# Attention in a four-layer kernel: q and k turned once and gathered by DMA, outputs moved by DMA in turned form

## The chip, the cores and the metric

One core of a Trainium2 chip runs the whole program. The metric is the device time of one execution in microseconds (us); the number for a kernel is the median of its runs.

## The reference, cut to what matters

The program chains a mixture-of-experts layer, an attention layer, a second mixture-of-experts layer, a sparse feed-forward layer, a state-space layer ("ssm" in the names) and a second sparse feed-forward layer on 1024 tokens of width 256. The change touches the attention and the preparation of the state-space layer.

```python
# attention on normalized x: 32 query heads, 8 key/value heads, head width 8
q = x @ Wq.T ; k = x @ Wk.T ; v = x @ Wv.T
q, k = rope(q, k)
scores = einsum('bkgqd,bkld->bkgql', q, k) * 8 ** -0.5
attn = softmax(scores, axis=-1)
out = einsum('bkgql,bkld->bkgqd', attn, v)
x = x + out.reshape(b, s, 256) @ Wo.T
```

## The kernel before

`attention_layer` (L597) works on 8 tiles of 128 tokens. Every product of q and k is made in split precision: a value is a high part (rounded for TensorE) and a low part, and both stand as rows of one operand, so that a contraction over 32 rows (`STACK`) gives hi·hi + lo·hi + hi·lo and, for the second pass, minus the row maximum (its two parts meet rows of −1 in k). Two heads lie in 64 rows; in `kz` ("k_picks") the rows of the head that is not wanted are zero.

Preparation: TensorE projects a tile, VectorE applies the rotation (L846 to L850), ScalarE copies the rounded parts into `q_stack` and `k_stack` (`stack_high`, L948), GpSimd subtracts the low parts (L781, L783). k is turned for all heads at once (L1037) and copied to `kT` (L960).

The main part goes over 8 groups (one key/value head and its 4 query heads each), written out for groups 0 and 7 and as a loop for 1 to 6. A group has 16 slots. In a slot TensorE issues, in this order: two transposed score matmuls (`scoresT`, L1103) into one pair of banks, two score chunks (L1087), two `scoresT` into the other pair, one chunk, the four value matmuls of the slot before (`values`, L1115), one chunk. ScalarE takes the exponential of each pair (L981, two of 128x1024 per slot). VectorE takes the row maximum of each chunk (`reduce`, L863), 4 a slot; these belong to rows that are needed later, since the second pass needs the maximum of the first. The chunks run ahead: `LEAD` = 40 chunks of group 0 are made before slot 0, and each group makes the rest of its own and the first 40 of the next. Chunks and turned things share a ring of three PSUM banks, given out by the table `bank_of`; TensorE waits until the holder of a bank is read.

In each group six jobs of four 128x128 transposes stand in that order too (`slot_jobs`, inserted as fourth job, behind the value matmuls): "q1" at slots 3 and 4 (L1063: the next group's q for the score chunks, copied by ScalarE, L965), "q2" at slots 6 and 14 (L1063: q with its maxima, copied by L969), and "o" at slots 1 and 9 (L1123: the output of half a group back to token order; VectorE then takes reciprocals of the sums, L871, and multiplies, L876). GpSimd splits the maxima into two parts (L804, L806) and copies each group's q (L787). SyncE gathers a group's k with 4 DMAs (L755). After group 7 the outputs are turned once more, split, projected with `w_o` and added (`turn_final`, `project_final`, L1135 to L890).

In `prepare` of the state-space layer each of 8 groups has two convolutions; ScalarE does the first tap (L1509), VectorE three more (L1514), TensorE the projections of the next group (L62 to L64), for which ScalarE rounds the weights (`high`, L1712) and GpSimd subtracts (`low`, L1641).

## Time and profile before

| what | value |
|---|---|
| median of 3 runs | 1743.71 us (1729.76 to 1744.64) |
| the profiled execution's own time | 1740.03 us |
| its span in the trace | 1738.2 us |
| mean granted TensorE clock | 0.932 of full speed |
| TensorE / VectorE / ScalarE / GpSimd busy | 86 / 62 / 50 / 28 % of the span |

All times in the trace count from the span's start. The attention runs from 193 to 674 us, the preparation of the state-space layer from 961 to 1066 us. A row of the timeline joins neighbouring instructions of one group (its count stands behind x); in square brackets stands how long the engine was idle before it and what ended that.

### The profile page before, as it was taken

The page shows a single profiled execution, that of the slowest core. Times are in us where ns is not written, and L with a number is a line of the kernel's source. Part 1 is how long each engine was busy: PE and PEld are TensorE (multiplying, and loading weights), DVE is VectorE, ACT ScalarE, POOL GpSimd, SP SyncE. Part 2 cuts the span into 40 slices and gives each one's busy share as a digit, 9 for nine tenths or more (in the row PEclk, how much of TensorE's full clock was granted, in tenths as well). Part 3 has the DMA queues.
Part 4 walks back from the last instruction along what each step waited for, and adds up shares of the span by engine and source line. Part 5 has one row for each costly group of instructions (what it writes and reads, how often), then busy time and mean ns, then how long its engine had stood idle before and what let it go on. Part 6 is the DMA issues. An engine that isn't in the chain of part 4 may idle for free. (4 is left out here: it accounts for less than half of the span.)

```text
span 1738.2 us, 24514 instructions
## 1 busy us (share of the span) xinstructions
PE 1488.4 (86%) x7880; PEld 1033.9 (59%) x7880; DVE 1080.0 (62%) x1948; ACT 877.6 (50%) x1268; POOL 493.8 (28%) x422
## 2 busy tenths in 40 slices
PE   3999479899998996799499787799999999999697
PEld 2566343333333334466277675688888888888586
DVE  4121577787888754212277665778777777878375
ACT  1222226676676673122143566666766666675332
POOL 1344320000000000244210112466565555565200
PEclk7999759999999997799799898999999999999799
DMA  8432210000000004623400111223232222331200
GB/s 299 122 49 40 50 25 1 13 13 12 12 12 0 12 1 153 216 43 49 104 11 1 43 34 49 88 76 100 70 99 92 73 91 73 102 93 46 76 1 25
DMA packets 78526, 107.33 MB, mean 62 GB/s; under 512 B 9600, under 2 KB 57984, under 8 KB 78432
## 3 DMA queue, kind: packets, MB, share of 16 engines
q1 hardware_dynamic: 69056, 91.98, 16.8%
q0 software_dynamic: 9376, 14.16, 4.6%
q8 instruction: 51, 0.84, 0.2%
q14 instruction: 43, 0.35, 0.1%
HBM read 89.99 MB, written 11.93 MB: 59 GB/s over the span
## 5 line engine op out<-in xcount | busy, mean ns | idle before, releaser
L981 ACT ACTIVATE attn_probs<-attn_scoresT 128x1024 f32<-128x1024 f32 x256 | 253.3, 1024 | 101.5 <-PE attn_scoresT L1103 99.0
L863 DVE TENSOR_REDUCE attn_max_chunks<-attn_scores 128x1 f32<-128x512 f32 x349 | 227.7, 685 | 48.7 <-PE attn_scores L1087 48.7
L1514 DVE SCALAR_TENSOR_TENSOR ssm_scan_x<-ssm_scan_proj,ssm_w_conv,ssm_scan_x 128x1023 f32<-128x1023 f32 (+2 forms) x96 | 123.0, 1282 | 80.8 <-ACT ssm_scan_x L1509 75.0
L1087 PE MATMUL attn_scores<-attn_k_picks,attn_qT_pass 64*128 64x512 f32 x349 | 149.8, 473 | 25.8 <-DVE attn_max_chunks L863 17.0
L1103 PE MATMUL attn_scoresT<-attn_qT_pass,attn_k_picks 64*128 64x512 f32 x512 | 163.9, 438 | 0.7 <-ACT attn_probs L981 0.7
L401 DVE TENSOR_TENSOR moe_h<-moe_silu,moe_up 128x512 f32<-128x512 f32 x46 | 31.6, 688 | 189.4 <-PE moe_up L516 189.4
L1115 PE MATMUL attn_o<-attn_probs,attn_v_group 128*32 128x512 f32 x1024 | 139.0, 615 | 0.9 <-ACT attn_probs L981 0.8
L1087 PEld LDWEIGHTS attn_scores<-attn_k_picks,attn_qT_pass 64*128 64x128 f32 x349 | 63.0, 192 | 122.6 <-DVE attn_max_chunks L863 98.2
L448 ACT ACTIVATE moe_silu<-moe_gate 128x512 f32<-128x512 f32 x46 | 27.5, 598 | 200.4 <-PE moe_gate L516 200.4
L62 PE MATMUL ssm_scan_proj<-ssm_xnT_hi,ssm_w_in_hi 128*128 128x512 f32 x256 | 108.7, 425 | 23.0 <-DVE ssm_scan_x L1514 21.0
L286 POOL DMA_INDIRECT moe_sums<-moe_y,moe_token x46 | 72.8, 1583 | 165.6 <-DVE moe_y L410 159.4
L2351 PE MATMUL ssm_scan_out<-ssm_scan_w_out,ssm_scan_v 128*128 128x256 f32 x480 | 113.5, 391 | 4.6 <-POOL ssm_scan_w_out L2056 4.4
L863 DVE TENSOR_REDUCE attn_max_chunks<-attn_turn 128x1 f32<-128x512 f32 x139 | 94.5, 680 | 28.0 <-PE attn_turn L1087 28.0
L64 PE MATMUL ssm_scan_proj<-ssm_xnT_hi,ssm_w_in_lo 128*128 128x512 f32 x256 | 102.6, 401 | 0.0
L2351 PEld LDWEIGHTS ssm_scan_out<-ssm_scan_w_out,ssm_scan_v 128*128 128x128 f32 x480 | 92.3, 197 | 17.2 <-POOL ssm_scan_w_out L2056 4.6
L63 PE MATMUL ssm_scan_proj<-ssm_xnT_lo,ssm_w_in_hi 128*128 128x512 f32 x256 | 102.3, 399 | 0.0
L804 POOL TENSOR_TENSOR attn_q_group<-attn_max,attn_zeros 128x16 fp32r<-128x16 f32 x16 | 3.6, 228 | 336.3 <-DVE attn_max L857 336.3
L2241 ACT ACTIVATE ssm_scan_gate<-ssm_scan_v 128x1024 f32<-128x1024 f32 x24 | 25.4, 1058 | 137.7 <-DVE ssm_scan_v L2134 137.7
L2034 POOL TENSOR_TENSOR ssm_scan_c_exp_cum<-ssm_cT,ssm_scan_exp_cum 128x896 f32<-128x896 f32 x32 | 70.8, 2212 | 80.9 <-PE ssm_scan_y L2325 79.5
L516 PE MATMUL moe_gate<-moe_w_gate_up,moe_xT 128*128 x184 | 90.3, 614 | 1.3 <-ACT moe_xT L442 1.3
L546 PE MATMUL moe_out<-moe_w_down,moe_hT 128*128 x368 | 87.1, 380 | 1.5 <-ACT moe_hT L454 1.5
L2042 POOL TENSOR_TENSOR ssm_scan_x_to_end<-ssm_scan_x_dt,ssm_decay_to_end 128x512 f32<-128x512 f32 x64 | 87.6, 1387 | 1.8 <-DVE ssm_scan_x_dt L2098 1.8
(337 smaller groups left out, 3415.2 us busy)
## 6 DMA issues: line engine op xcount, KB each, us to landing
ssm_cum_all<-ssm_cums SPq DMA_DIRECT2D x32, 512.0 KB, 3.8
ssm_scan_exp_cum<-ssm_cums SPq DMA_DIRECT2D x32, 512.0 KB, 3.7
moe_w_gate_up<-in_moe_w SPq DMA_DIRECT2D x16, 512.0 KB, 10.8
moe_w_up<-in_moe_w SPq DMA_DIRECT2D x16, 512.0 KB, 10.9
moe_w_down<-in_moe_w SPq DMA_DIRECT2D x16, 512.0 KB, 11.1
ssm_w_in<-in_in_w SPq DMA_DIRECT2D x64, 128.0 KB, 2.6
attn_k_picks<-attn_kT SPq DMA_DIRECT2D x32, 128.0 KB, 2.4
ssm_scan_w_out<-in_out_w SPq DMA_DIRECT2D x8, 512.0 KB, 3.9
```

The source lines that it names most:

```text
L62: nc.tensor.matmul(out, lhs_hi, rhs_hi, start=start, stop=False)
L63: nc.tensor.matmul(out, lhs_hi, rhs_lo, start=False, stop=False)
L64: return nc.tensor.matmul(out, lhs_lo, rhs_hi, start=False, stop=stop)
L516: last = nc.tensor.matmul(bank[:].unsqueeze(1), xT[i % 2][:, k, :], w_in[name][:, bass.ds(e * KD + k, 1), :], start=(k == 0), stop=(k == K ...
L863: return nc.vector.tensor_reduce(rmaxc[:, half, place:place + 1], chunk_bank(g, n), AX_X, ALU.max).then_inc(reduced, 1)
L981: nc.scalar.activation(probs[s % 2][:, 2 * pair:2 * pair + 2, :], st_ps[pair][:], ACT.Exp, scale=SCALE).then_inc(exp_done, 1)
L1087: nc.tensor.matmul(chunk_bank(g, n), qm[b][head_rows(j), t * P:(t + 1) * P], kz[b][head_rows(j), j % 2, c * BANK:(c + 1) * BANK], start=Tr ...
L1103: last = nc.tensor.matmul(st_ps[pair][:, i, :], kz[b][head_rows(j), j % 2, kt * P:(kt + 1) * P], qe[b][head_rows(j), half * BANK:(half + 1 ...
L1115: last = nc.tensor.matmul(o_ps[j * STACK:(j + 1) * STACK, :], vg[b][:, kt, :], probs[s % 2][:, i, :], start=(kt == 0), stop=(kt == KT_TILE ...
L1514: return nc.vector.scalar_tensor_tensor(out[:, shift:], ps[:, :S - shift], w(k), out[:, shift:], ALU.mult, ALU.add)
L2042: nc.gpsimd.tensor_tensor(xend[:, cs, :], xdt[:, cs, :], to_end[:, cs, bass.ds(n, 1)] .broadcast_to([P, cs.stop - cs.start, PD]), ALU.mult ...
L2351: last = nc.tensor.matmul(out[:, m, :], v[:, v_row(b * NORM_HEADS + jn), cols], w_out[:, jn, :], start=(jn == 0), stop=(jn == NORM_HEADS - 1))
```

## The change

q and k are turned to `[head rows, tokens]` once, in the preparation, straight from the rotated tiles (`turn_roped`, three transposes a tile), rounded and split there by half of the tokens (`turned_high`, `turned_late` on ScalarE, `turned_parts` on VectorE, one subtraction on GpSimd). SyncE then gathers a group's rows with DMAs: 12 for k, 6 for q, and 2 that clear the rows of the maxima (`load_group`). The two passes use one operand `qs` ("q_group"); the maxima alone are turned in the loop, as one transpose of 128x32 (`turn_max`), copied by VectorE (`copy_max`) and put into `qs` by two DMAs (`load_max`). The outputs stay turned: ScalarE copies them to `oT`, and 8 DMAs of 8 rows each (`send_out`) put values and sums into `o_all` and `o_sums`. The division is done at the end, for 4 blocks of 128x512 (or 96x512): reciprocal and rounding on VectorE, product and low part on GpSimd; the last group still goes by the old way. `LEAD` becomes 44, the order of chunks within a half changes, and the slots of the last projections move from 13 and 14 to 11 and 13. In `prepare` of the state-space layer `high` of the next group stands before the `silu` and the second tap.

```diff
 TURNS = (0, 2, 1, 3)
-FINAL_SLOTS = (11, 12)
 PER_SLOT = CHUNKS // SLOTS
-LEAD = HALF + 2 * PER_SLOT
+LEAD = HALF + 3 * PER_SLOT
 LEAD_SCORES_T = 36
+LEAD_MAX = LEAD_SCORES_T + 2
+OWN_TOP_SLOT = (CHUNKS - LEAD) // PER_SLOT - 1
+NEXT_TOP_SLOT = (CHUNKS + HALF - LEAD) // PER_SLOT - 1
+FINAL_SLOTS = (11, 13)
+LAST_ROWS = 3 * STACK
...
+            c, r = divmod(r, HALF // 2)
+            return TURNS[r % GQ], half * (TT // 2) + r // GQ, c
...
-            if s in Q1_SLOTS:
-                jobs.insert(3, ("q1", 1, Q1_SLOTS.index(s)))
-            if s == KT_TILES - 2:
-                jobs.insert(3, ("q2", 0, 1))
-            if s == SLOTS - 2:
-                jobs.insert(3, ("q2", 1, 0))
-            if s == 1:
-                jobs.insert(3, ("o", -1, 1))
-            if s == KT_TILES + 1:
-                jobs.insert(3, ("o", 0, 0))
+            if s == OWN_TOP_SLOT + 1:
+                jobs.append(("max", 0, 1))
+            if s == NEXT_TOP_SLOT + 1:
+                jobs.append(("max", 1, 0))
             return jobs
...
+            def load_group(g):
+                b = g % 2
                 if g >= 2:
                     sync.wait_ge(scoresT_done, 2 * SLOTS * (g - 1))
+                if g >= 4:
+                    sync.wait_ge(hi_done, 6)
+                    sync.wait_ge(q1_lo, 2)
+                load_k(g, kT_hi, (0, 1), slice(0, S), kz_in[b])
+                load_k(g, kT_lo, (3,), slice(0, S), kz_in[b])
+                load_q(g, qT_hi, (0, 3), slice(0, S), q_in[b])
+                load_q(g, qT_lo, (1,), slice(0, S), q_in[b])
+                if g >= 2:
+                    for w in range(2):
+                        at = w * SPAN + STACK
+                        sync.dma_start(f32(qs[b][at:at + 4, :]), none[:]).then_inc(q_in[b], 16)
+
+            def load_max(g, half):
+                sync.wait_ge(m_copied, 2 * g + half + 1)
+                for w in range(2):
+                    at = w * SPAN + STACK
+                    sync.dma_start(f32(qs[g % 2][at:at + 4, half_cols(half)]),
+                                   f32(topsT[half][w * 16:(w + 1) * 16, :])).then_inc(max_in[half], 16)
+
+            def send_out(g, half):
+                sync.wait_ge(o_copied, 2 * g + half + 1)
                 for j in range(GQ):
-                    src = (g % 4) * STACK
-                    sync.dma_start(f32(kz[g % 2][j * STACK:(j + 1) * STACK, j % 2, :]),
-                                   f32(kT[src:src + STACK, g // 4, :])).then_inc(kz_in[g % 2], 16)
+                    row = g % 4 * STACK + j * HD
+                    for dst, at in ((o_all, j * STACK), (o_sum, j * STACK + HD)):
+                        sync.dma_start(dst[row:row + HD, g // 4, half_cols(half)], oT[half][at:at + HD, :]
+                                       ).then_inc(o_out[half], 16)
+
...
+                load_q(0, qT_lo, (1,), half_cols(half), q_first[half])
+            load_max(0, 0)
+            for g in range(KV):
+                if g < KV - 1:
+                    load_group(g + 1)
+                if g:
+                    send_out(g - 1, 1)
+                load_max(g, 1)
+                if g < KV - 1:
+                    send_out(g, 0)
+                    load_max(g + 1, 0)
...
+                half, k = divmod(u, KD)
+                rows, cols = slice(0, LAST_ROWS if k else P), half_cols(half)
+                pool.wait_ge(rec_done, u + 1)
+                nc.gpsimd.tensor_tensor(o_all[rows, k, cols], o_all[rows, k, cols], o_sum[rows, k, cols], ALU.mult
+                                        ).then_inc(prod_done, 1)
+                pool.wait_ge(prod_hi, u + 1)
+                nc.gpsimd.tensor_tensor(oT_lo[rows, k, cols], o_all[rows, k, cols], f32(oT_hi[rows, k, cols]), ALU.subtract
...
+                dve.wait_ge(m_turned, 2 * g + half + 1)
+                if not (isinstance(g, int) and g == 0):
+                    dve.wait_ge(max_in[half], 32 * g)
+                nc.vector.tensor_copy(topsT[half][:], max_bank(g, half)[0:STACK, 0:P]).then_inc(m_copied, 1)
+
+            def reciprocals(k, half):
+                rows, cols = slice(0, LAST_ROWS if k else P), half_cols(half)
+                dve.wait_ge(o_out[half], 16 * 2 * GQ * (KV - 1))
+                nc.vector.reciprocal(o_sum[rows, k, cols], o_sum[rows, k, cols]).then_inc(rec_done, 1)
...
+                dve.wait_ge(prod_done, KD * half + k + 1)
+                nc.vector.tensor_copy(oT_hi[rows, k, cols], o_all[rows, k, cols]).then_inc(prod_hi, 1)
...
+            def last_slot(s):
+
+                if s == OWN_TOP_SLOT + 2:
+                    reciprocals(0, 0)
+                    reciprocals(1, 0)
+                    high_parts(0, 0)
+                    high_parts(1, 0)
+                if s == KT_TILES + 1:
+                    last_outputs(0)
+                if s == KT_TILES + 2:
+                    last_low(0)
+                    reciprocals(0, 1)
+                    high_parts(0, 1)
+                if s == KT_TILES + 4:
+                    reciprocals(1, 1)
+                    high_parts(1, 1)
...
+            def turned_high(half):
+                rows, cols = slice(0, KV * HD), half_cols(half)
+                act.wait_ge(turned, 3 * half + 1)
+                nc.scalar.copy(kT_hi[:, cols], k_bank[half][rows, :]).then_inc(hi_done, 1)
+                act.wait_ge(turned, 3 * half + 2)
+                nc.scalar.copy(qT_hi[:, 0, cols], q_bank[half]).then_inc(hi_done, 1)
...
+                if not (isinstance(g, int) and g == 0):
+                    act.wait_ge(o_out[half], 16 * 2 * GQ * g)
+                nc.scalar.copy(oT[half][:], o_ps[:]).then_inc(o_copied, 1)
...
+                pe.wait_ge(roped_done, t + 1)
+                parts = ((k_bank[half][0:KV * HD, cols], roped[:, t, HEADS * HD:]), (q_bank[half][:, cols], roped[:, t, 0:P]),
+                         (q1_bank[half][:, cols], roped[:, t, P:2 * P]))
+                for dst, src in parts:
+                    last = nc.tensor.transpose(dst, src, ident)
+                    if t % 4 == 3:
...
+            def turn_max(g, half):
                 pe.wait_ge(top_split, 2 * g + half + 1)
-                turn_q(q2_bank(g, half), b, half, q2_turned)
-
...
+            def group_ready(g, b):
+                pe.wait_ge(kz_in[b], 96 * g if b == 0 else 96 * (g - 1) + 192)
+                pe.wait_ge(q_in[b], 64 * g if b == 0 else 64 * (g - 1) + 96)
...
+                            turn_o(0)
+                        if s == KT_TILES + 2:
+                            turn_final(0)
                         for p in range(2):
                             if s == FINAL_SLOTS[p]:
-                                turn_final(p)
-                            if s == FINAL_SLOTS[p] + 2:
                                 project_final(p)
...
             def body(g, b):
                 first, last = edge(g)
                 tap(g, 0)
+                if not last:
+                    high(g + 1, 1 - b)
                 if not first:
                     silu(g - 1, 1 - b, 1)
                 tap(g, 1)
-                if not last:
```

On TensorE, one slot of group 1 with a turn. Before, slot 3 (L1063 is the "q1" job, `attn_turn` the third bank of the ring):

```order
L1087 MATMUL attn_scores<-attn_k_picks,attn_qT_pass_1 128x512
L1109 REGISTER_ALU
L1115 MATMUL attn_o<-attn_probs,attn_v_group 32x512 x4
L1047 REGISTER_ALU
L1068 REGISTER_ALU
L1063 MATMUL attn_turn<-main_ident,attn_q_group 128x128 x4
L1047 REGISTER_ALU
L1087 MATMUL attn_scores<-attn_k_picks,attn_qT_pass_1 128x512
L1099 ISA
L1103 MATMUL attn_scoresT<-attn_qT_pass_1,attn_k_picks 128x512 x2
```

And in the changed kernel, slot 5, the first of the two slots of a group in which something is turned (`attn_max_parts` are the split maxima):

```order
L1147 MATMUL attn_scores<-attn_k_picks,attn_q_group 128x512
L1169 REGISTER_ALU
L1175 MATMUL attn_o<-attn_probs,attn_v_group 32x512 x4
L1116 REGISTER_ALU
L1147 MATMUL attn_scores<-attn_k_picks,attn_q_group 128x512
L1116 REGISTER_ALU
L1126 REGISTER_ALU
L1127 MATMUL attn_scores<-main_ident,attn_max_parts 32x128
L1159 ISA
L1163 MATMUL attn_scoresT<-attn_q_group,attn_k_picks 128x512 x2
```

Four transposes between the value matmuls and the fourth chunk have become one, behind the fourth chunk; the slots with "q1" and "o" turn nothing now.

On SyncE, what the whole attention issues before:

```order
L743 DMA attn_w_qkv<-in_w_qkv 128x2x384
L744 DMA attn_cos<-in_cos 128x8x4
L745 DMA attn_sin<-in_sin 128x8x4
L746 DMA attn_w_o<-in_w_o 128x2x256
L755 DMA attn_k_picks<-attn_kT 32x1024 x32
```

And in the changed kernel, the start of what it issues for group 1 (the load of group 2, then the outputs of half a group):

```order
L749 DMA attn_k_picks<-attn_kT_hi 8x1024 x8
L749 DMA attn_k_picks<-attn_kT_lo 8x1024 x4
L757 DMA attn_q_group<-attn_qT_hi 16x1024 x4
L757 DMA attn_q_group<-attn_qT_lo 16x1024 x2
L774 DMA attn_q_group<-attn_no_max 4x1024 x2
L788 DMA attn_o_all<-attn_oT 8x512
L788 DMA attn_o_sums<-attn_oT 8x512
```

The last two stand four times; then come the 2 DMAs of the maxima (L780), again 8 of outputs and 2 of maxima: 40 a group where there were 4.

On ScalarE, one group of the state-space preparation (group 2), before:

```order
L1509 ACTIVATE ssm_prep_conv<-ssm_prep_proj,ssm_b_conv,ssm_w_conv 128x1024
L1749 ACTIVATE ssm_prep_cT_first<-ssm_prep_conv 128x128
L1750 ACTIVATE ssm_cT<-ssm_prep_conv 128x896
L1509 ACTIVATE ssm_prep_conv<-ssm_prep_proj,ssm_b_conv,ssm_w_conv 128x1024
L1712 CAST ssm_prep_w_bc_hi<-ssm_prep_w_bc 128x512
```

and in the changed kernel:

```order
L1572 ACTIVATE ssm_prep_conv<-ssm_prep_proj,ssm_b_conv,ssm_w_conv 128x1024
L1775 CAST ssm_prep_w_bc_hi<-ssm_prep_w_bc 128x512
L1812 ACTIVATE ssm_prep_cT_first<-ssm_prep_conv 128x128
L1813 ACTIVATE ssm_cT<-ssm_prep_conv 128x896
L1572 ACTIVATE ssm_prep_conv<-ssm_prep_proj,ssm_b_conv,ssm_w_conv 128x1024
```

The rounding of the next group's weights has moved past the second tap and the two `silu` instructions.

## Rows read from the trace of the kernel before

**Rows 1.** Stretches: length, busy PE, PEld, DVE, ACT, POOL, PEclk, DMA share, GB/s.

```profile
232.00:258.00 26.00, 21.52 (x43) 10.36 (x43) 22.45 (x39) 1.46 (x2) 1.66 (x3) 0.50 0.08 17
310.00:360.00 50.00, 45.12 (x279) 17.68 (x271) 40.36 (x69) 34.58 (x38) 2.36 (x6) 1.00 0.05 11
```

**Rows 2.** Timeline of group 0: value matmuls (L1115) and a "q1" turn.

```profile
270.83 1.06 PE L1115 MATMUL attn_o<-attn_probs,attn_v_group 128*32 128x512 f32 x8
271.83 0.66 PE L1063 MATMUL attn_turn<-main_ident,attn_q_group 128*128 128x128 f32 x4
274.73 1.06 PE L1115 MATMUL attn_o<-attn_probs,attn_v_group 128*32 128x512 f32 x8
...
278.61 1.07 PE L1115 MATMUL attn_o<-attn_probs,attn_v_group 128*32 128x512 f32 x8
281.31 1.07 PE L1115 MATMUL attn_o<-attn_probs,attn_v_group 128*32 128x512 f32 x8
```

**Rows 3.** Timeline: an "o" turn, and the same slot a group later.

```profile
290.23 1.06 PE L1115 MATMUL attn_o<-attn_probs,attn_v_group 128*32 128x512 f32 x8
...
295.01 1.07 PE L1115 MATMUL attn_o<-attn_probs,attn_v_group 128*32 128x512 f32 x8
...
345.88 1.07 PE L1115 MATMUL attn_o<-attn_probs,attn_v_group 128*32 128x512 f32 x8
```

**Rows 4.** Groups by shape: busy us, mean ns of one, idle before.

```profile
L981 ACT ACTIVATE attn_probs<-attn_scoresT 128x1024 f32<-128x1024 f32 x256 | 253.3, 1024 | 101.5 <-PE attn_scoresT L1103 99.0
L863 DVE TENSOR_REDUCE attn_max_chunks<-attn_scores 128x1 f32<-128x512 f32 x349 | 227.7, 685 | 48.7 <-PE attn_scores L1087 48.7
...
L871 DVE RECIPROCAL attn_recip<-attn_scores 128x16 f32<-128x16 f32 x15 | 3.7, 249 | 8.0 <-PE attn_scores L1123 8.0
...
L316 DVE RECIPROCAL moe_rstd<-moe_std 128x4 f32<-128x4 f32 x4 | 0.7, 178 | 2.3 <-ACT moe_std L427 2.3
```

**Rows 5.** Line L755, the gather of k: issue ns min/median/max, and landing.

```profile
L755 SPq DMA_DIRECT2D attn_k_picks<-attn_kT x32: 507/591/1600, 227.8 to 567.0; - x32
...
DMA to landing us min/median/max: 2.3/2.4/3.5
```

**Rows 6.** Timeline of the preparation and the lead of the attention.

```profile
210.05 0.49 DVE L850 TENSOR_TENSOR attn_roped<-attn_qk_cos,attn_qk_sin 128x320 f32<-128x320 f32 x1
...
211.35 0.73 POOL L783 TENSOR_TENSOR attn_q_stack<-attn_roped,attn_q_stack 128x256 f32<-128x256 f32 x1
211.44 0.99 DVE L850 TENSOR_TENSOR attn_roped<-attn_qk_cos,attn_qk_sin 128x320 f32<-128x320 f32 x1
...
227.77 5.03 SPq L755 DMA_DIRECT2D attn_k_picks<-attn_kT  x8
...
232.94 2.48 DVE L863 TENSOR_REDUCE attn_max_chunks<-attn_scoresT 128x1 f32<-128x512 f32 x4 [9.16 <-PE attn_scoresT L1087]
...
258.69 1.12 PE L1103 MATMUL attn_scoresT<-attn_qT_pass,attn_k_picks 64*128 64x512 f32 x2
```

**Rows 7.** Timeline of group 7 (two slots with chunks) and of the tail.

```profile
632.95 1.07 PE L1115 MATMUL attn_o<-attn_probs,attn_v_group 128*32 128x512 f32 x8
636.26 1.07 PE L1115 MATMUL attn_o<-attn_probs,attn_v_group 128*32 128x512 f32 x8
...
666.40 1.07 ACT L987 CAST attn_xnT_hi<-attn_scores 128x512 fp32r<-128x512 f32 x2 [2.08 <-PE attn_scores L1135]
```

**Rows 8.** Groups of instructions, state-space preparation, 1005 to 1064 us: busy, mean ns, idle before.

```profile
L62 PE MATMUL ssm_prep_proj<-ssm_xnT_hi,ssm_prep_w_bc_hi 128*128 128x512 f32 x43 | 17.9, 417 | 7.8 <-POOL ssm_prep_w_bc_lo L1641 6.2 <-DVE ssm_prep_conv L1514 1.6
```

**Rows 9.** Timeline of one group of that preparation.

```profile
1016.71 6.74 DVE L1514 SCALAR_TENSOR_TENSOR ssm_prep_conv<-ssm_prep_proj,ssm_w_conv,ssm_prep_conv 128x1022 f32<-128x1022 f32 x5 [0.15 <-DVE ssm_prep_conv L1514]
...
1018.48 0.60 ACT L1712 CAST ssm_prep_w_bc_hi<-ssm_prep_w_bc 128x512 fp32r<-128x512 f32 x1
1019.16 1.27 POOL L1641 TENSOR_TENSOR ssm_prep_w_bc_lo<-ssm_prep_w_bc,ssm_prep_w_bc_hi 128x512 fp32r<-128x512 f32 x1 [8.75 <-ACT ssm_prep_w_bc_hi L1712]
1020.57 0.50 PE L62 MATMUL ssm_prep_proj<-ssm_xnT_hi,ssm_prep_w_bc_hi 128*128 128x512 f32 x1 [1.60 <-POOL ssm_prep_w_bc_lo L1641]
```

More of the change, by code:

```diff
@@ L837, in _, with rope @@
             dve.wait_ge(tab_in, 32)
-            for t in range(TT):
+            def rope(t):
                 b = t % 2
@@ L1003, in body @@
                         copy_o(g, 0)
-                    for p in range(2):
-                        if last and s == FINAL_SLOTS[p]:
-                            turned_high(p)
-            for half in range(2):
-                copy_q1(0, 0, half)
-            act.wait_ge(wo_in, 16)
-            nc.scalar.copy(wo_hi[:], wo_raw[:]).then_inc(wh, 1)
-            copy_q2(0, 0, 0)
+                    if last and s == KT_TILES + 1:
+                        last_high(0)
             groups(act, body)
             copy_o(KV - 1, 1)
-            for p in range(2, 4):
-                turned_high(p)
+            last_high(1)
         @block.tensor
@@ L1020, in _, with turn_roped @@
             ln.tensor(nc, ident)
+            def turn_roped(t):
+                half, cols = t // 4, slice(t % 4 * P, (t % 4 + 1) * P)
+                pe.wait_ge(roped_done, t + 1)
[4 more added lines that the diff above has]
+                    if t % 4 == 3:
+                        last.then_inc(turned, 1)
             pe.wait_ge(wl, 1)
@@ L1206, in _ @@
             values(KV - 1, 1, SLOTS - 1)
-            turn_o(KV - 1, 1)
-            for p in range(2, 4):
-                turn_final(p)
+            turn_o(1)
+            turn_final(1)
             for p in range(2, 4):
```

451 lines of the change are left out of this document (223 added, 228 removed).

## The prediction

> **What bounds the kernel now.** I read the page first, then the busy time by stretch, then the timeline of TensorE in the attention, slot by slot, and last the timelines of its preparation, its tail and the state-space preparation. A bound of about 1% of this kernel (17 us) is what its measurement can tell from no change.
>
> The loop of the attention is the largest piece. In a stretch of 50 us TensorE is busy 45.12 us at full granted clock, VectorE 40.36, ScalarE 34.58 [rows 1]. TensorE sets the pace, and what it does besides the real work is to be seen in the starts of the value matmuls. A slot without a turn takes 281.31 − 278.61 = 2.70 us. A slot with a "q1" turn takes 274.73 − 270.83 = 3.90, 1.20 more, although its four transposes are 0.66 us of work [rows 2]: the bank that is held until ScalarE has copied it costs the rest. The "o" turn at slot 9 makes 295.01 − 290.23 = 4.78, 2.08 more, as the bank is held until two VectorE steps are done. The same slot comes again at 345.88, so a group lasts 50.87 us, of which 16 x 2.70 = 43.20 are plain slots and 7.67 the six turns [rows 3]. The other turned slots (0.8 to 1.2 us extra each) are in that difference.
>
> In the preparation VectorE's addition of the rotated parts takes 0.49 us alone and 0.99 when GpSimd subtracts beside it (0.73, at 211.35); the gather of k begins at 227.77, the first row maximum at 232.94, and the lead of 40 chunks goes at VectorE's pace, (2.48 − 0.69)/3 = 0.60 us each, the 0.69 being the last one's own length [rows 4, 6]. The first `scoresT` comes at 258.69 [rows 6]. In the state-space preparation TensorE waits for GpSimd's low parts: 6.2 us under that name and 1.6 under another, 5 waits of about 1.5 [rows 8]; the chain is rounding at 1018.48, subtraction at 1019.16 (1.27 long), projection at 1020.57 after 1.60 idle [rows 9].
>
> **The change part by part**, against the profiled execution's 1740.03 us (3.7 below the median of the runs, 1743.71).
>
> *Turns that go.* Groups 1 to 6 lose 7.67 us each, 46.0. Group 0 has no "o" at slot 1, whose price is like that of "q1", so it loses 7.67 − 1.20 = 6.5. Together −52.5. What is late next is the plain slot, 2.70, which VectorE (4 x 0.60 = 2.4 a slot) and ScalarE (34.58 of 50 us, less its copies) stay under.
>
> *The turns of the maxima.* 14 in groups 0 to 6, each one transpose (0.66/4 = 0.16 us of TensorE) and one VectorE copy out of PSUM of 128 columns, no dearer than its 16-column reciprocal plus a little, about 0.28. Bounds: 0.1 us where the slack hides them, 1.2 where one costs as much as a "q1" turn [rows 2]. Since both engines stand in the ring, I take 0.16 + 0.24 = 0.4: +5.6 (1.4 to 16.8).
>
> *SyncE's queue.* It had 4 DMAs a group and gets 40, and this is the wait that could replace the turns. An issue of k's gather cost 0.51 to 1.60 us, median 0.59, landing 2.4 us later [rows 5]; eight in a row took 5.03 [rows 6], 0.63 each with the gap of 0.04, so the cheapest would be 0.55. The load of group g+1 may start when the last `scoresT` of g−1 is done, some 1.7 us before slot 0 of g. The first chunk that reads it stands in slot 5, 1.7 + 5 x 2.70 = 15.2 us later. 20 issues at 0.63 and the landing make 12.6 + 2.4 = 15.0; at 0.55 they make 13.4. Then 8 DMAs of outputs end at 17.6 at the latest, the maxima are copied at about 18.4 (start of slot 6), their two DMAs are issued by 19.7 and landed by 22.1; `scoresT` wants them in slot 8, at 23.3. The second pair (copied at slot 14, wanted at 16) has the same 2 slots, and the queue is free. So it fits by 0.2 and 1.2 us at the dear price. I take 0, bounds 0 and +6 (1 us in each of six loads). An issue price of 0.9 us is a rival below.
>
> Transfers of 32 KB are what the Trainium skill warns of ("DMA: Bandwidth & Descriptors", section Bandwidth: under 64 KB the descriptors dominate). No row here shows a DMA of 8 rows; by the rule the transfers would be slow for their bytes, which matters only if the landing grows beyond the 2.4 us of the sum.
>
> *Preparation and lead.* GpSimd subtracts nothing during the rotations, so the additions fall from 0.99 to 0.49, 7 of them: −3.5; two splits of VectorE (at most 0.69 each, as a row maximum over as many columns) come in between: +1.4. Rotations 1.39 apart (211.44 − 210.05) bring tile 3 at 210.05 + 3 x 1.39 = 214.2, and with its turn, behind the projection of tile 5, and the rounding the first gather starts at about 216.5. It has 18 issues, 9.9 to 11.3 us, then 2.4: first chunk at 228.8 to 230.2, first row maximum 0.8 later, against 232.94 [rows 6]. The second half's gather takes as long again and ends at 238.7 to 241.5, just when chunk 16 is due. Chunk 38 waits for the copy of the first maxima, 1.4 + 0.2 + 38 x 0.60 later, and those need two issues and a landing (3.6): the first `scoresT` comes at 257.9 to 259.3, against 258.69, with 44 chunks done by then. I take −0.5 (−4 to +3).
>
> The Trainium skill ("SBUF — State Buffer", section Who interferes with whom) says that a VectorE instruction with two SBUF inputs and a GpSimd instruction that reads SBUF exclude each other. By that rule the additions here would all be 0.49; 0.49 and 0.99 in the trace agree [rows 6].
>
> *Group 7 and the tail.* Gone: "o" at slot 1 (−1.2), the two chunk slots of 636.26 − 632.95 = 3.31 us, which had lost the order's missing "q1" banks (−1.2 for both against 2.70), one slot of chunks (−0.4), in the tail half of the copy that took 1.07 for two and about as much of the subtraction behind it (−1.1) [rows 7]. New: one maxima turn (+0.4), and one stall. ScalarE's `last_high(0)` stands in its slot 9, but TensorE makes what it waits for at the end of slot 10, behind value matmuls (1.06) and four transposes (0.66) [rows 2]; the exponentials of slot 10 queue behind it, and `scoresT` behind them. With the copy (about 0.6, from 1.07 for two) that is some 2.5 us. The new reciprocals of 128x512 are long: from 16 and 4 columns, (249 − 178)/12 = 5.9 ns a column [rows 4], so 178 + 508 x 5.9 = 3.2 us each, four of them, and four products on GpSimd at about 1.3, as its subtraction of that shape [rows 9]. They begin at slot 6; the first two blocks are ready some 10 us later, in slot 10 or 11 by slots of two exponentials (2 x 1.02 us [rows 4]) and a copy now and then; the first projection is due at the end of slot 11. So they just fit. Sum −1.0, bounds −5 and +5.
>
> The Trainium skill ("VectorE: DVE Perf Modes", section First, the fixed hardware budget) says that a reciprocal repeats its divide step 8 times. Were that 8 of its cycles a column at the 0.96 GHz of that page of the skill, one would be an estimated 4.4 us and the stall in slot 10 would grow by some 2 us; the trace's 5.9 ns a column does not bear it out.
>
> *State-space preparation.* Rounding moves from behind ScalarE's second tap to behind its first, which is done before 1016.71, so at least 1.8 us sooner than 1018.48, and the low parts are ready before their bank. Then the bank decides: VectorE's five instructions from 1016.71 are 6.74/5 = 1.35 apart, the second ends the first convolution, at about 1019.35 [rows 9], and the projection can follow, 1.2 us before 1020.57. So 5 x 1.2 = −6.0, bounds −8 (all of the waits, 7.8) and −2.
>
> Sum: −52.5 + 5.6 + 0 − 0.5 − 1.0 − 6.0 = −54.4, that is 1685.6 for a profiled execution; the median of runs lies between this and 3.7 more. I say 1686.
>
> **The rivals.**
> *SyncE late by a little.* Eight-row DMAs cost 0.9 us each to issue, between the median and the largest of rows 5. The load is then 18 + 2.4 = 20.4 against 15.2, 5 us late in six groups: +30, 1716. For it: 36 further issues a group and one queue. Against: even DMAs of 32 rows took 0.59, and eight in a row were 0.63 apart [rows 5, 6].
> *SyncE late by much (slower).* At 1.6 us an issue, the largest seen [rows 5], 40 issues are 64 us a group, and the group lasts that long instead of 43.6: 7 x 20.4 = +143, 1829. It turns into a loss once a group lasts about 51.8 us, which is at 1.3 us an issue by the queue's whole length, and at about 1.1 by the way from the load to the first maxima (28 issues). Against: 1.60 was the largest of 32, the median 0.59.
> *The plain slot stretches.* The maxima's turn, the changed order of chunks, or VectorE's copy brings TensorE and VectorE out of step, and slots cost 2.90: 0.2 x 16 x 7 = +22, 1708. For it: VectorE is at 2.4 of 2.70, so a small delay shows. Against: plain slots follow each other at 2.70 already.
> *The turns were not the price.* If the time of a turned slot were VectorE's backlog, only half of it would go: +26, 1712. Against: 64 x 0.60 = 38.4 us is all VectorE needs for chunks in a group of 50.87.
>
> **How the numbers follow.** The forecast has 0.73, the small SyncE case 0.10, the stretched slot 0.08, the half gain 0.05, the slower one 0.03, no case 0.01. The bounds of the unknown terms, taken together and not all at one end, give 1673 to 1701 for the forecast alone. The range reaches to the cases at 1708 and nearly to that at 1712: 1671 to 1710. Faster by over 1% (below 1726): all but the slower case and a rest, 0.95; within 1%: 0.02; slower 0.03.
>
> **What would show it.** Right: value matmuls 2.70 us apart through whole groups, a group of 43.5 to 44.5 us, no DMA among what ends TensorE's idle time in slots 5, 8 and 0; rotations 1.4 us apart; first `scoresT` near 258; the state-space projections no longer waiting for GpSimd, each group about 1.2 us shorter. Wrong: L1147 waiting for the DMAs of L749 or L757, L1163 waiting for those of L780, SyncE's issues over 0.63 us apart; reciprocals over 4 us and the last group's projections waiting for them; slots of 2.9.

## The result, and the profile after

The changed kernel takes 1677.33 us (median of 4 runs, 1675.31 to 1684.23) against 1739.30 for the kernel before (median of 4 runs): ratio 0.966, 95% interval 0.960 to 0.971. The forecast was 1686 with 1671 to 1710. The profiled execution took 1684.23 us, the longest of the four, 55.8 less than that of before.

Where it came from is seen from the starts of each layer's first DMA on SyncE. The last line is the mean of the ten other kernels below that leave the later layers as they are in the changed one, for the layers that they don't touch:

| us | first MoE | attention | second MoE | FFN | ssm preparation | ssm scan | last FFN |
|---|---|---|---|---|---|---|---|
| before | 182.1 | 482.2 | 185.3 | 101.1 | 108.5 | 563.1 | 100.3 |
| after | 185.0 | 430.7 | 184.4 | 101.1 | 100.4 | 564.6 | 100.8 |
| mean of ten | 182.3 | | 184.1 | 100.3 | 103.5 | 560.9 | 101.0 |

The attention gave 51.5 us. The first mixture-of-experts layer and the scan, untouched, vary by 5 us from execution to execution, so a difference of a few us is read from its own layer below and not from the whole. How far such a reading holds is seen from "ssm_back" below, whose attention is that of the changed kernel: 431.1 us against 430.7.

The loop, a stretch of 50 us: the same columns as [rows 1], and the starts of value matmuls in group 0, as [rows 2]:

```profile
310.00:360.00 50.00, 48.55 (x296) 18.62 (x294) 46.40 (x78) 36.90 (x40) 1.34 (x6) 1.00 0.19 30
```

```profile
278.29 1.06 PE L1175 MATMUL attn_o<-attn_probs,attn_v_group 128*32 128x512 f32 x8
281.22 1.06 PE L1175 MATMUL attn_o<-attn_probs,attn_v_group 128*32 128x512 f32 x8
283.93 1.07 PE L1175 MATMUL attn_o<-attn_probs,attn_v_group 128*32 128x512 f32 x8
...
324.95 1.06 PE L1175 MATMUL attn_o<-attn_probs,attn_v_group 128*32 128x512 f32 x8
```

TensorE is busy 48.55 of 50 us (45.12 before). A slot with a maxima turn takes 2.93 us, a plain one 2.71, and the same slot comes again after 324.95 − 281.22 = 43.73 us instead of 50.87 [rows 3]: 16 x 2.70 and two turns of 0.25. All groups look like this.

The lines of the gather and of the maxima on SyncE (issue ns min/median/max), and the turn of the maxima:

```profile
L749 SPq DMA_DIRECT2D attn_k_picks<-attn_kT_hi x72: 624/625/668, 219.5 to 528.7; - x72
...
L757 SPq DMA_DIRECT2D attn_q_group<-attn_qT_hi x36: 535/588/600, 224.9 to 533.9; - x36
...
DMA to landing us min/median/max: 1.9/2.0/2.0
...
L780 SPq DMA_DIRECT2D attn_q_group<-attn_maxT x32: 647/660/714, 258.5 to 586.2; - x32
...
L1127 PE MATMUL attn_scores<-main_ident,attn_max_parts x16: 269/285/393, 256.6 to 584.8; 128*32 128x128 f32 x16
...
L924 DVE CAST attn_maxT<-attn_scores x16: 265/268/279, 258.2 to 585.2; 32x128 fp32r<-32x128 f32 x16
```

An 8-row DMA costs 0.625 us to issue (0.67 with the gap), a 16-row one 0.59, and the landing is 2.0 us after the issue (second and third row). TensorE's weight loads waited for L780 once, 0.8 us, at the first maxima of all, and 0.2 us once for a load.

The preparation, against [rows 6]. The layer began 2.7 us later than before (at 195.66 against 192.96):

```profile
201.79 6.02 DVE L118 TENSOR_SCALAR attn_xn<-main_residual,attn_ln_mean_var,attn_ln_rstd 128x256 f32<-128x256 f32 x4
...
207.93 1.38 DVE L118 TENSOR_SCALAR attn_xn<-main_residual,attn_ln_mean_var,attn_ln_rstd 128x256 f32<-128x256 f32 x4
...
219.54 5.31 SPq L749 DMA_DIRECT2D attn_k_picks<-attn_kT_hi  x8
...
233.24 0.79 PE L1147 MATMUL attn_scoresT<-attn_k_picks,attn_q_group 64*128 64x512 f32 x2 [7.09 <-DMA attn_q_group<-attn_qT_lo]
...
261.56 1.11 PE L1163 MATMUL attn_scoresT<-attn_q_group,attn_k_picks 64*128 64x512 f32 x2
```

The first `scoresT` comes 65.9 us after the layer's start, 65.7 before. Two things stand out. The first four normalizations take 6.02 us and the next four 1.38, and TensorE waits 7.09 us at the end of SyncE's 18 issues in a row.

Group 7, slots 10 and 11 (start of value matmuls to start), then the two stretches behind slot 10 with the columns of [rows 1]:

```profile
594.35 1.06 PE L1175 MATMUL attn_o<-attn_probs,attn_v_group 128*32 128x512 f32 x8
...
596.48 0.58 ACT L1064 CAST attn_xnT_hi<-attn_scores 32x512 fp32r<-32x512 f32 x1 [2.67 <-PE attn_scores L1195]
...
597.81 3.35 DVE L929 RECIPROCAL attn_o_sums<-attn_o_sums 128x512 f32<-128x512 f32 x1
598.15 0.19 PEld L1163 LDWEIGHTS attn_scoresT<-attn_q_group,attn_k_picks 64*128 64x128 f32 x2 [1.95 <-ACT attn_probs L1059]
...
599.50 1.82 PE L1175 MATMUL attn_o<-attn_probs,attn_v_group 128*32 128x512 f32 x8
...
604.35 1.06 PE L1175 MATMUL attn_o<-attn_probs,attn_v_group 128*32 128x512 f32 x8
```

```profile
599.50:604.35 4.85, 4.85 (x27) 2.75 (x25) 3.46 (x3) 1.48 (x3) 2.55 (x2) 0.65 0.00 0
604.35:612.24 7.89, 7.14 (x51) 3.00 (x49) 3.69 (x4) 6.07 (x7) 2.56 (x2) 1.00 0.01 2
```

Slot 10 lasts 5.15 us, as ScalarE stood 2.67 us before the rounding and its exponentials behind it. Slot 11 lasts 4.85 us although TensorE is busy throughout: after the idle time its granted clock was 0.65 on average, most of the slot at 1.2 instead of 2.4 GHz. In the 7.89 us behind it the clock is whole again.

### The profile page after: what moved, and what is told of

The parts are those of the page before. It is cut to its first block and busy times, and to the rows that moved or that the text cites. A ratio compares the mean times of both kernels' runs of the same rounds, so it can differ in the third digit from the quotient of the medians.

```text
span 1682.4 us, 24339 instructions
## 1 busy us (share of the span) xinstructions
PE 1460.8 (87%) x7712; PEld 1021.4 (61%) x7712; DVE 1089.4 (65%) x1946; ACT 846.8 (50%) x1206; POOL 489.9 (29%) x409
## 5 line engine op out<-in xcount | busy, mean ns | idle before, releaser
L918 DVE TENSOR_REDUCE attn_max_chunks<-attn_scores 128x1 f32<-128x512 f32 x488 | 305.4, 684 | 23.9 <-PE attn_scores L1147 23.8
L1059 ACT ACTIVATE attn_probs<-attn_scoresT 128x1024 f32<-128x1024 f32 x256 | 247.9, 1022 | 122.3 <-PE attn_scoresT L1163 122.1
L1147 PE MATMUL attn_scores<-attn_k_picks,attn_q_group 64*128 64x512 f32 x488 | 185.8, 462 | 10.9 <-DVE attn_max_chunks L918 2.3
L1147 PEld LDWEIGHTS attn_scores<-attn_k_picks,attn_q_group 64*128 64x128 f32 x488 | 85.0, 190 | 173.2 <-DVE attn_max_chunks L918 164.8
L1163 PE MATMUL attn_scoresT<-attn_q_group,attn_k_picks 64*128 64x512 f32 x512 | 151.7, 433 | 3.3 <-ACT attn_probs L1059 3.3
L546 PEld LDWEIGHTS moe_out<-moe_w_down,moe_hT 128*128 128x128 f32 x368 | 69.8, 190 | 30.2 <-issue 23.1
L845 POOL TENSOR_TENSOR attn_max_parts<-attn_max,attn_zeros 128x16 fp32r<-128x16 f32 x16 | 3.6, 224 | 287.8 <-DVE attn_max L913 287.8
## 6 DMA issues: line engine op xcount, KB each, us to landing
moe_w_up<-in_moe_w SPq DMA_DIRECT2D x16, 512.0 KB, 11.2
moe_w_down<-in_moe_w SPq DMA_DIRECT2D x16, 512.0 KB, 11.5
```

The source lines that it names most:

```text
L546: last = nc.tensor.matmul(out_ps[i % 2][:, 0:D].unsqueeze(1), hT[i % 2][:, k, :], w_dn[:, bass.ds(e * KI + k, 1), :], start=(k == 0), stop ...
L918: return nc.vector.tensor_reduce(rmaxc[:, half, place:place + 1], chunk_bank(g, n), AX_X, ALU.max).then_inc(reduced, 1)
L1059: nc.scalar.activation(probs[s % 2][:, 2 * pair:2 * pair + 2, :], st_ps[pair][:], ACT.Exp, scale=SCALE).then_inc(exp_done, 1)
L1147: nc.tensor.matmul(chunk_bank(g, n), qs[b][head_rows(j), t * P:(t + 1) * P], kz[b][head_rows(j), j % 2, c * BANK:(c + 1) * BANK], start=Tr ...
L1163: last = nc.tensor.matmul(st_ps[pair][:, i, :], kz[b][head_rows(j), j % 2, kt * P:(kt + 1) * P], qs[b][head_rows(j), half_cols(half)], sta ...
```

## The experiments

### What a turned slot costs, and why

Four unread transposes were put back at slots 2 and 10 of groups 0 to 6, as fourth job:

```diff
+            if s in (2, 10):
+                jobs.insert(3, ("extra", 1, (2, 10).index(s)))
...
-            free_from[bank] = k + 3
+            free_from[bank] = k + (5 if job[0] == "extra" else 3)
...
+                for t in range(4):
+                    last = nc.tensor.transpose(bank[:, t * P:(t + 1) * P], roped[:, t, 0:P], ident)
```

In "turn_held" ScalarE copies the bank and its next user waits for that; in "turn_free" nobody does.

> The changed kernel with four 128x128 transposes put back at slots 2 and 10 of groups 0 to 6 (14 in all), between the value matmuls and the fourth chunk, into a bank of the ring that stays held until ScalarE has copied it, as the old q1 turn did; their result is used by nothing. Theory (a turn costs its 0.66 us of work and the rest because one of three banks is held): such a slot lasts 3.9 us instead of 2.70, so 14 x 1.2 = +16.8 us against the changed kernel. Rival (turned slots were slow from VectorE's backlog, which the changed order of chunks has removed): VectorE is unchanged at 2.4 us a slot, so no more than the 0.66 us of work shows, at most +9.

> The same 14 sets of four transposes in the same places and banks, but nobody copies them and the next chunk may take the bank at once. Theory of the held bank: only the work is left, 0.66 us each, slots of 3.36 us, +9.2 us against the changed kernel and 7.6 us less than with the copy. Rival (the price is the break in the order that puts TensorE and VectorE out of step, whoever holds the bank): slots of 3.9 us as with the copy, +16.8 us.

Measured: 1699.17 us (1695.86 to 1711.20) and 1705.11 (1702.70 to 1707.41), but the attention layers last 451.1 and 450.8 us, +20.4 and +20.2: the same. The two profiled executions are 9.2 us apart, of which 3.1 lie in the first MoE, 5.0 in the scan and 1.6 in the state-space preparation, none of which the edit touches. The 14 turned slots take 3.88 us each in both, +16.5; another 3.2 come from slot 15 of each group, which turns nothing and grew from 2.70 to 3.16. The added jobs shift the order of the banks, but no run tries whether that is why. A turned slot of the run without a copy:

```profile
315.83 1.07 PE L1184 MATMUL attn_o<-attn_probs,attn_v_group 128*32 128x512 f32 x8
...
318.70 0.50 PE L1156 MATMUL attn_scores<-attn_k_picks,attn_q_group 64*128 64x512 f32 x1 [0.55 <-DVE attn_max_chunks L920]
...
319.71 0.64 PE L1184 MATMUL attn_o<-attn_probs,attn_v_group 128*32 128x512 f32 x4
```

3.88 us, and the 0.55 of waiting for VectorE [rows 2] is there without any copy. So my reason for the 1.2 us was wrong, at least as I put it. What both runs share is the table, which keeps the bank from the next five jobs. Two more runs change only that number: "turn_reuse" is the run without a copy with `k + 1`, "turn_hold3" the one with the copy with `k + 3`. And "before_hold3" is the kernel before with one edit:

```diff
-            free_from[bank] = k + (3 if job[0] == "chunk" else 5)
+            free_from[bank] = k + (5 if job[0] == "o" else 3)
```

> The 14 unread sets of four transposes again, but now the table that gives out the three banks counts the bank as free for the very next job instead of five jobs later. Theory (what a turn costs beyond its work is the bank that is missing from the ring for five jobs, and it is the table that keeps it away, not the copy, which is why the run without the copy was no faster): slots of 3.3 us, 14 x 0.6 = +8 us in the attention stage against the changed kernel, instead of +20.2. Rival (VectorE idles 0.6 us while TensorE transposes and TensorE then waits for it, whichever bank is taken): slots of 3.9 us again, +16 to +20 us.

> As the run with ScalarE's copy, but the table holds the bank of the turn for three jobs, as it holds that of a chunk. Theory: the copy is done 1.3 us after the last transpose starts, before the third job wants the bank, so the ring keeps its three banks and only the 0.6 us of work is left, slots of 3.3 us, +8 us in the attention stage. Rival (a bank whose reader is ScalarE, behind its exponentials, really is needed for five jobs): TensorE waits for the copy, slots of 3.9 us or more, +16 us or more.

> The kernel before, with one number changed: q1 and q2 turns hold their bank for three jobs in the table instead of five (o turns keep five). Theory of the table: each of the 28 q turns loses the 0.55 us that TensorE waited for VectorE, about -15 us against the kernel before, a group lasts about 48.7 us instead of 50.87. Rival (the five jobs were right for these turns): no change, or slower, as TensorE then waits for ScalarE's copy.

| | median us (range) | attention | turned slot |
|---|---|---|---|
| turn_reuse | 1692.03 (1691.32 to 1692.77) | 443.7 | 3.29 |
| turn_hold3 | 1687.19 (1684.56 to 1690.38) | 440.2 | 3.28 |
| before_hold3 | 1716.48 (1712.40 to 1718.07) | 458.0 | "q" 3.29, "o" 3.88 |

One turned slot of "turn_hold3", and the "o" slot of "before_hold3" one group apart:

```profile
311.94 1.06 PE L1190 MATMUL attn_o<-attn_probs,attn_v_group 128*32 128x512 f32 x8
...
315.22 1.06 PE L1190 MATMUL attn_o<-attn_probs,attn_v_group 128*32 128x512 f32 x8
```

```profile
313.84 1.06 PE L1115 MATMUL attn_o<-attn_probs,attn_v_group 128*32 128x512 f32 x8
...
361.77 1.07 PE L1115 MATMUL attn_o<-attn_probs,attn_v_group 128*32 128x512 f32 x8
```

What TensorE waited for from the first value matmul on (us in total, times, longest), in the kernel before and in "before_hold3":

```profile
PE attn_scores L1087 <- DVE attn_max_chunks L863: 16.2, 30, 0.5
PE attn_turn L1087 <- DVE attn_max_chunks L863: 8.1, 15, 0.6
PE attn_scores L1087 <- DVE attn_xn L876: 5.4, 7, 0.8
```

```profile
PE attn_turn L1087 <- DVE attn_max_chunks L863: 4.4, 8, 0.6
PE attn_scores L1087 <- DVE attn_max_chunks L863: 3.8, 7, 0.5
```

For the "q" turns the table is the cause. A turn adds 0.58 us; the other 0.6 was the wait of 0.55 us for VectorE that comes with two banks instead of three, and the third was missing because the table said five jobs, not because ScalarE needed them. The kernel before with this one number is 1.4% faster (ratio 0.986, 0.981 to 0.990), its group 361.77 − 313.84 = 47.93 us instead of 50.87, and its attention layer 24.2 us shorter. That is 9 more than I expected of it, and the slots say where it lies: the "q" slots of seven groups gave 14.1 us, slot 9 gave 6.3 (4.79 to 3.88, TensorE's seven waits for VectorE's `xn` are gone), two chunk slots of group 7 gave 1.2, and two losses of clock, described next, did not come, 2.8. The "o" turn at slot 1 stayed at 3.88. So nearly half of the 51.5 us could be had without moving anything. Whether the "o" turns need their five jobs was not tried.

"turn_reuse" and "turn_hold3" lie above their +8 as well, at +13.0 and +9.5 us of attention layer. The turned slots are as expected, 14 x 0.59 = 8.3. The rest of "turn_reuse" is slot 15 again (3.17, in all 3.2 us) and 1.5 us at the end of the layer; in "turn_hold3" slot 15 takes 2.94 (1.7 us in all).

The kernel before, two stretches of the same group (columns as in [rows 1]) behind its "o" turn at slot 9:

```profile
396.90:399.80 2.90, 2.90 (x13) 1.03 (x14) 0.81 (x2) 0.00 (x0) 0.00 (x0) 0.50 0.00 0
399.90:402.80 2.90, 2.90 (x21) 1.15 (x17) 2.68 (x5) 2.12 (x3) 0.00 (x0) 1.00 0.00 0
```

After the two waits of that slot (0.55 us for VectorE's maximum and 0.77 for its `xn`) TensorE's clock was granted at 0.50 for 2.9 us, 13 matmuls instead of 21. It happened in two of the seven groups of that execution (here and at 601.7) and made slots of 5.05 and 3.87 us out of 4.79 and 2.70, 1.4 us each time. The other five groups had the same waits and kept the clock.

### How full SyncE's queue is

```diff
+                    for n in range(2):
+                        sync.dma_start(spare[b][4 * n:4 * n + 4, :], none[:]).then_inc(q_in[b], 16)
```

stands behind the clears of `load_group`; "clears6" has `range(6)`, and `group_ready` waits for them too.

> Two more 4-row DMAs (into rows that nothing reads) at the end of each of the six loads of groups 2 to 7, waited for with the load; SyncE is then 1.34 us later at 0.67 us an issue. Theory (the load just fits, its slack is about zero, since a chunk already waited 0.2 us for it once): slot 5 grows by about 1.2 us in six groups, +7 us against the changed kernel. Rival (there is slack that the trace does not show, as the score banks between TensorE and VectorE take up a late chunk): +0 to +2 us.

> Six more such DMAs a load, 4.0 us of SyncE. Theory (slack about zero): +3.8 us in each of six groups, +23 us. Rival (hidden slack of 1 us or more): +18 us or less; the difference to the run with two more gives the price of one issue, and the crossing with zero gives the slack. Third possibility (only the queue's total length counts, 46 x 0.67 = 31 us of 43.7): no change in either run.

Measured: 1683.18 us (1681.59 to 1686.37), attention 432.8, +2.1; and 1717.72 (1714.15 to 1720.53), attention 466.9, +36.3. The waits of TensorE in the loop, by what they were for (us in total, times, longest), of "clears2" and of "clears6", and then three stretches of "clears6":

```profile
PE attn_scores L1150 <- DMA attn_spare<-attn_no_max: 2.3, 6, 0.8
```

```profile
PE attn_scores L1150 <- DMA attn_spare<-attn_no_max: 17.9, 6, 3.7
```

```profile
319.90:324.81 4.91, 4.91 (x18) 1.91 (x17) 2.76 (x6) 1.95 (x3) 0.00 (x0) 0.50 0.09 17
324.81:328.68 3.87, 3.87 (x18) 1.54 (x17) 2.32 (x4) 1.55 (x2) 0.00 (x0) 0.56 0.02 6
331.37:334.07 2.70, 2.61 (x18) 1.01 (x17) 2.49 (x5) 2.50 (x5) 0.00 (x0) 1.00 0.00 0
```

In "clears2" the median is 5.9 us above that of the changed kernel, which would fit the +7, but the six slots that first read a new load grew by only 0.17 to 0.71 us, 1.8 in all, where the theory had 1.2 each. The slack: these issues are 0.585 us (0.63 with the gap), so two make 1.27 and six 3.8 us. Of 6 x 1.27 = 7.6 us, 2.3 became waiting, of 22.7, 17.9: both leave 0.8 to 0.9 us of slack per load. My sum had 0.2, and the rival of the first run was right. But the second run is far above both figures given for it. Its 17.9 us of waiting are only half of the 36.3. In the three stretches shown, two slots behind the first wait and a later one, the clock was granted at 0.50, then 0.56, then 1.00, and the two slots took 4.91 and 3.87 us instead of 2.95 and 2.70, 3.1 us. So it went in four of the six groups; in the other two the slots behind lost 2.6 and 0.8 us. That is some 16 us, and the slots of the waits themselves, partly at the lower clock, hold the other 3. The waits of 0.2 to 0.8 us of "clears2" cost no clock.

### The state-space preparation

```diff
-                if not last:
-                    high(g + 1, 1 - b)
                 if not first:
                     silu(g - 1, 1 - b, 1)
                 tap(g, 1)
+                if not last:
+                    high(g + 1, 1 - b)
```

> The changed kernel with the rounding of the next group's weights put back behind the second tap in the state-space preparation. Theory (the whole of the 8.1 us by which that stage became shorter in the profiles comes from this line): the stage lasts 107.6 us again, +8 us against the changed kernel, TensorE waits for GpSimd's low parts again. Rival (part of it is the spread between executions): the stage grows by less, 2 to 5 us.

Measured: 1686.10 us (1684.53 to 1688.63), the stage 109.9 us, against 108.5 and 110.0 for the two kernels with the old order and 100.4 to 104.8 (mean 103.2) for eleven profiles with the new one: 6.3 us between the means, less than the +8 and more than the rival's 2 to 5. What TensorE waited for in this run and in the changed kernel:

```profile
L62 PE MATMUL ssm_prep_proj<-ssm_xnT_hi,ssm_prep_w_bc_hi 128*128 128x512 f32 x48 | 20.1, 418 | 7.8 <-POOL ssm_prep_w_bc_lo L1704 6.2 <-DVE ssm_prep_conv L1577 1.6
```

```profile
L62 PE MATMUL ssm_prep_proj<-ssm_xnT_hi,ssm_prep_w_bc_hi 128*128 128x512 f32 x46 | 19.1, 416 | 1.7 <-DVE ssm_prep_conv L1577 1.6
```

The wait for the low parts is back to the tenth [rows 8] and the one for the bank stays, as predicted. The 8.1 us between the first two profiles seems to be in part their clock: the granted clock over the stage was 0.91 in the profile after, the shortest of the eleven, and 0.87 in that of "clears2", the longest with 104.8.

### Three places that the profile after points to

```diff
-                    if last and s == KT_TILES + 1:
+                    if last and s == KT_TILES + 2:
                         last_high(0)
```

```diff
             split(0, w_hi, w_lo, w_raw)
+            pool.wait_ge(ln.xn_done, TT)
             nc.gpsimd.memset(f32(kz[1][:]), 0.0).then_inc(kz_clear, 1)
```

The third, "q_pool", takes `load_q` out of SyncE's preparation for group 0 and issues the same DMAs with `nc.gpsimd.dma_start`, behind the same waits.

> ScalarE's rounding of the first half of the last group's outputs moves from slot 9 behind the exponentials of slot 10. Theory (the exponentials of slot 10 were stuck behind it, 2.9 us, and the idle TensorE then lost its clock, 1.6 us more in the next slot): slot 10 falls from 5.15 to 2.3 to 2.6 us and slot 11 from 4.85 to 3.3, together -4.4 us. Rival (the wait only moves to the projection at the end of slot 11, which needs VectorE's low part, 2 us later than now): -1 us or nothing.

> GpSimd clears the second k buffer, the q buffers and v's padding only after VectorE has normalized all tokens. Theory (the first four normalizations took 6.02 us and the next four 1.38, because GpSimd's memsets ran beside the first four): the first four fall to 1.4 us, or to about 3 where GpSimd's subtraction still runs beside them, and everything up to the first gather is 3 to 4.6 us sooner: -3 to -4.6 us. Rival (the clears now end late, and the DMAs of minus ones and the first gather wait for them, or the memsets slow the rotation instead): 0 to +2 us.

> In the preparation the 12 DMAs of group 0's q are issued by GpSimd, SyncE keeps the 24 of k. Theory (TensorE's 7.1 us of waiting before the first chunk is SyncE's 18 issues in a row): six fewer in front, the first chunk is 18 x 0.67 - 12 x 0.67 = 4 us sooner, -3.6 us in all. Rival (GpSimd's DMAs take longer, 1.0 us to issue and 9.8 us to land in the mixture-of-experts layer): 6 x 1.0 + 9.8 = 15.8 us after q is turned at 219.9, that is 235.7 instead of 233.2, +2 to +3 us.

| | median us (range) | attention | against 430.7 |
|---|---|---|---|
| last_high | 1676.44 (1671.87 to 1678.46) | 426.9 | −3.7 |
| memsets | 1676.37 (1671.96 to 1679.53) | 426.9 | −3.8 |
| q_pool | 1675.26 (1674.22 to 1676.74) | 429.0 | −1.7 |

By the whole time none of the three is told from the changed kernel (1677.33, 1675.31 to 1684.23), so they are read from their slots and stages. In "last_high" slots 10 and 11 take 2.68 and 3.29 us at full clock (5.15 and 4.85 in the changed kernel), −4.0; both in one stretch:

```profile
591.97:597.94 5.97, 5.60 (x42) 2.82 (x41) 4.08 (x5) 4.45 (x6) 1.70 (x2) 1.00 0.00 0
```

In "memsets" both sets of normalizations take 1.38 us:

```profile
199.23 1.38 DVE L118 TENSOR_SCALAR attn_xn<-main_residual,attn_ln_mean_var,attn_ln_rstd 128x256 f32<-128x256 f32 x4
...
202.18 1.81 POOL L824 MEMSET attn_k_picks<- 128x2048 f32 x1 [2.92 <-DVE attn_xn L118]
```

The Trainium skill ("SBUF — State Buffer", section Who interferes with whom) has this: a `tensor_scalar` may run in a mode that takes the port pair shared with GpSimd, and then whichever of the two issues first blocks the other, while an instruction with at most one input in SBUF outside that mode is not touched. The times agree: 6.02 beside the clears and 1.38 without, while a multiplication of the rotation (PSUM and SBUF) took 0.49 beside the same clears and 0.48 behind them. Which mode ran, no trace shows.

In "q_pool" the first gather starts 23.5 us after the layer's start and the first `scoresT` 61.4 (65.9 in the changed kernel), −4.5 us: GpSimd issued each DMA in 0.5 us and it landed in 2.0 (its line first, then one row of VectorE's timeline and one stretch of the tail).

```profile
L829 POOL DMA_DIRECT2D attn_q_group<-attn_qT_hi x8: 484/514/582, 217.0 to 226.3; - x8
...
DMA to landing us min/median/max: 1.8/2.0/2.6
```

```profile
219.50 2.22 DVE L907 TENSOR_TENSOR attn_roped<-attn_qk_cos,attn_qk_sin 128x320 f32<-128x320 f32 x1
```

```profile
612.00:616.00 4.00, 4.00 (x20) 4.00 (x20) 0.69 (x1) 0.00 (x0) 0.00 (x0) 0.50 0.00 0
```

One addition of the rotation took 2.22 us beside GpSimd's issues and subtraction. The rest of the gain went to the clock at the other end: in this execution the projections of the tail ran at 0.50 (last row; in the profile after, the same work ran at 1.00), 2.7 us more, and slots 10 and 11 took 11.2 instead of 10.0.

Waits of the same length cost clock in one execution and none in another. "memsets" has the stall of slot 10 as the changed kernel has it (5.15 us). Its slot 11 and its projections at the end, with the columns of [rows 1]:

```profile
593.21:596.50 3.29, 3.29 (x27) 1.95 (x25) 1.90 (x2) 1.47 (x3) 1.28 (x1) 1.00 0.00 0
611.11:615.60 4.49, 4.49 (x24) 4.39 (x24) 0.69 (x1) 0.00 (x0) 0.00 (x0) 0.62 0.00 0
```

Slot 11 kept its clock and took 3.29, but the projections ran at 0.62 and the tail, from the last value matmul to the next layer, took 15.6 us instead of 14.1. Of the ten profiles with that stall, four are like the changed kernel (slot 11 at 4.75 to 4.85, tail 14.1), three like "memsets" (3.29 and 15.6), and three lost clock in both places. The tail has idle time of its own before the projections, and the next run, which has no stall in slot 10, lost clock there too, so the loss in the tail isn't shown to come from the stall.

All three together:

> The changed kernel with the three single edits together: ScalarE's rounding one slot later in the last group, GpSimd's clears after the normalization, the 12 first DMAs of q issued by GpSimd. Theory (they lie in different places of the path, so they add up): attention stage 430.7 - 3.7 - 3.8 - 4.5 = 418.7 us, the time 12 us under the changed kernel, about 1665 us. Rival (with the clears late GpSimd's queue holds up its own DMAs, or the gains overlap in the preparation): attention stage 421 to 424 us.

Measured: 1669.46 us (1665.14 to 1669.86), ratio to before 0.959 (0.954 to 0.963), attention 419.2 us, 11.5 under the changed kernel: the edits add up where they act. Up to the first value matmul the layer is 8.4 us shorter (3.9 in "memsets" and 4.5 in "q_pool"), slots 10 and 11 are 4.0 shorter as in "last_high", and the first slot 0.9 as in "q_pool"; the tail lost 1.9 to the clock (15.9 us). The intervals of the two ratios overlap, so by the whole time alone the order of the two isn't settled; by the layer it is.

## Why the prediction was right

*Turns that go* (−52.5): right in size, wrong in its reason. "The bank that is held until ScalarE has copied it costs the rest" fails: without the copy a slot is as long, and with it and a three-job hold it is 0.6 shorter. The 0.6 came from the table's five jobs, which left VectorE behind by 0.55 us a turn. The rival "the turns were not the price" fell as well, since four transposes put back made the 1.2 us again. From the first value matmul to the slot in which the changed kernel runs out of chunks (115 slots in both), the kernel before spent 58.8 us beyond 2.70 a slot and the changed one 4.6, a gain of 54.2 where my terms give 48.7. The rest is the two lost clocks (2.8 us), which I had not looked for because I took one group's 50.87 for all, and the next item.

*Turns of the maxima*: 0.24 us each, not 0.4. VectorE's copy (0.27 us, the estimate was 0.28) costs TensorE nothing, so only one engine's part counts: 3.4 instead of 5.6.

*SyncE*: 0, as forecast. The issue was dearer (0.67 against 0.63 with the gap) and the landing cheaper (2.0 against 2.4), and the slack was 0.8 to 0.9 instead of 0.2. My sum also laid the landing behind the end of the last issue, while it counts from its start: in "clears6" the last issue of group 1's load began at 316.1, and TensorE went on at 318.3.

*Preparation*: +0.2 for −0.5. Rotations 1.39 apart, as worked out; but the first four normalizations took 1.4 us more than before (6.02 against 4.62), since GpSimd has more to clear at the start, and the first chunk came 37.6 us after the layer's start where my sum had 35.8 to 37.2. (Its last line is off by 0.3 us as well: its terms give 257.6 to 259.0, not 257.9 to 259.3. And the group of 43.6 us in a rival should be 43.20 + 2 x 0.4 = 44.0. Neither changes a term or a chance.)

*Group 7 and tail*: the step that was mis-sized. Behind the last slots with chunks the changed kernel is 2.5 us slower (42.2 before, 44.7 after), where my terms for that part give +0.8. The stall of slot 10 is there with 2.9 for 2.5; what I left out is that it can take the clock down for the slot behind it: 1.6 us here, and 0.9 to 2.5 in seven of the ten profiles with that stall, nothing in three. The reciprocals took 3.34 us (estimate 3.2), GpSimd's products 1.28 (1.3), and nothing waited for them.

*State-space preparation*: −6.3 over all profiles for −6.0.

Sum for the profiled execution: 1685.6 forecast, 1684.23 measured, and that this is closer than the parts is luck: the loop was 5.5 us better, the tail 1.7 worse, the preparation 0.7 worse, the state-space preparation 2.1 better, and the first MoE layer and the scan, untouched, happened to be 2.9 and 1.5 us longer. The median is 9 us lower than forecast. Its executions have no profile, so where the rest lies is not shown; the ten other profiles have the first MoE layer and the scan together 6.4 us shorter than the profile after.

## What to carry to other kernels

Where a ring of buffers is given out by a table, the table's hold times are costs like any wait: test them one number at a time before rebuilding what the jobs do. Price a wait on TensorE with the clock behind it: here single waits of up to 0.8 us cost themselves, two in one slot (0.55 and 0.77) cost 1.4 us more in two of seven groups and nothing in five, and waits of about 3 us cost 1.5 to 2.3 times their length. And compare kernels layer by layer, since the layers nobody touched vary by more than a small edit is worth.

## What was not expected of the hardware

- After a wait of 2.8 to 3.7 us on TensorE the granted clock stood at 0.50 to 0.56 (the 1.2 GHz level, or mostly) for 8.8 us in four of six groups, and for less in the other two; after the shorter waits of one "o" turn in two of seven groups. Behind the stall in slot 10 of group 7 it fell in seven of ten profiles.
- An issue on SyncE isn't cheaper for fewer rows: 0.625 us for 8 rows, 0.59 for 16 and 32, 0.585 to 0.66 for 4. On GpSimd the same DMA took 0.51, with the same landing.
- Normalizing 128x256 took 1.5 us instead of 0.35 each beside GpSimd's memsets.
